# A fused cross-attention and 4-bit feed-forward kernel: order of loads, reciprocals and context transposes within a round

## The reference, cut to what matters

```python
def xattn(q, k, v, Wq, Wk, Wv, Wo, bo, g):            # q = layernorm(x), k = v = ctx, [32, 64, 512]
    qh, kh, vh = heads(Wq @ q), heads(Wk @ k), heads(Wv @ v)      # 8 heads of 64
    qh = softmax(qh, over the head's 64 rows) / 8
    kh = softmax(kh, over the 512 positions)
    context = kh @ vh.T                                # 64 x 64 for each head
    out = Wo @ (context.T @ qh) + bo
    return out / max(norm(out, over the 64 channels), 1e-12) * g * 8

def ffn(x):                                            # 512 -> 1376 -> 512, weights of 4 bits
    gate, up = x @ dequant(Wg), x @ dequant(Wu)
    return (silu(gate) * up) @ dequant(Wd)

x = x + tanh(g_xattn) * xattn(layernorm(x), ctx, ctx, ...)
x = x + tanh(g_ffn) * ffn(layernorm(x))
```

## Time and profile before

| | |
|---|---|
| device time, runs of before | 812.04, 816.8, 819.32 us (median 816.8) |
| the profiled execution | 815.45 us, span 813.7 us from first to last instruction |
| busy: PE, DVE, ACT, POOL | 731.1 us (90%), 612.2 (75%), 436.6 (54%), 186.2 (23%) |
| round 0 begins (first maxima) | at 13.39 us |
| round 1, 2, 3 begin | at 39.48, 65.00, 93.17 us |
| round 15 begins | at 436.31 us |
| feed-forward part, first product | at 523.65 us |
| mean granted TensorE clock | 0.977 of full speed |

### The profile page before, as it was taken

How to read it: one execution, slowest core, us unless ns; L and a number is a source line. 1 busy time by engine, 2 the same in 40 slices (tenths; PEclk the granted TensorE clock), 3 DMA queues, 4 the chain that set the end, 5 groups by cost and what they waited for, 6 DMA issues and landing times. The chain is left out here.

```text
span 813.7 us, 13752 instructions
## 1 busy us (share of the span) xinstructions
PE 731.1 (90%) x4551; PEld 392.8 (48%) x4551; DVE 612.2 (75%) x806; ACT 436.6 (54%) x764; POOL 186.2 (23%) x317
## 2 busy tenths in 40 slices
PE   4889988988998999999999966399999999999997
PEld 3544553554454455455545532135555555555555
DVE  6377776877878777787778554399988877877885
ACT  3766665665666667566665632144443445334443
POOL 5122222213213222321322211211121112211121
PEclk9999999999999999999999996599999999999999
DMA  3021312321330321122020000100000000100001
GB/s 99 9 76 32 81 23 67 81 50 37 80 82 5 82 67 26 48 67 69 11 63 18 5 6 1 63 10 1 1 1 27 27 0 13 39 0 0 26 26 52
DMA packets 29195, 29.89 MB, mean 37 GB/s; under 512 B 18628, under 2 KB 18756, under 8 KB 29036
## 3 DMA queue, kind: packets, MB, share of 16 engines
q1 hardware_dynamic: 26972, 28.85, 13.1%
q10 hardware_dynamic: 2192, 0.66, 0.3%
HBM read 23.49 MB, written 4.23 MB: 34 GB/s over the span
## 5 line engine op out<-in xcount | busy, mean ns | idle before, releaser
L1300 DVE SCALAR_TENSOR_TENSOR acc<-ffn_bank,scale_T,acc 128x512 f32<-128x512 f32 (+1 forms) x264 | 186.7, 748 | 39.6 <-PE ffn_bank L1253 34.1
L1252 PE MATMUL ffn_bank<-ek,w_gu 128*128 (+3 forms) x352 | 137.9, 392 | 2.8 <-PEq L90 1.8
L1253 PE MATMUL ffn_bank<-ekT,w_gu 128*128 (+3 forms) x352 | 134.4, 382 | 0.0
L1160 POOL TENSOR_TENSOR in_lo<-inter,in_hi 128x512 fp32r<-128x512 f32 (+1 forms) x44 | 56.4, 1282 | 229.9 <-ACT in_hi L1199 229.9
L1192 ACT ACTIVATE act_gate<-acc 128x512 f32<-128x512 f32 (+1 forms) x44 | 27.7, 630 | 144.3 <-DVE acc L1300 144.3
L985 DVE TENSOR_TENSOR eq<-eq,pair 128x1024 f32<-128x1024 f32 x64 | 78.0, 1220 | 25.1 <-PE pair L741 25.1
L493 ACT ACTIVATE eq<-pair 128x1024 f32<-128x1024 f32 x64 | 65.6, 1025 | 55.0 <-PE pair L761 55.0
L977 DVE TENSOR_REDUCE qmax<-pair 128x16 f32<-128x1024 f32 x64 | 77.6, 1212 | 14.9 <-PE pair L623 14.6
L484 ACT ACTIVATE ek<-pair,kneg 128x512 f32<-128x512 f32 x128 | 86.6, 685 | 3.6 <-DVE kneg L980 3.5
L1269 PE MATMUL ffn_bank<-wd_hi,in_hi 128*128 128x512 f32 (+1 forms) x176 | 86.7, 531 | 0.4 <-DVE wd_lo L1333 0.4
L1269 PE MATMUL ffn_bank<-wd_lo,in_hi 128*128 128x512 f32 (+1 forms) x176 | 86.7, 531 | 0.0
(11 more groups left out here) (138 smaller groups left out, 1168.7 us busy)
## 6 DMA issues: line engine op xcount, KB each, us to landing
xall<-in_x SPq DMA_DIRECT2D x16, 256.0 KB, 3.9
ctx_raw<-in_ctx SPq DMA_DIRECT2D x16, 256.0 KB, 4.1
out_x<-xall SPq DMA_DIRECT2D x16, 256.0 KB, 2.0
zero<-zeros_plus SPq DMA_DIRECT2D x8, 344.0 KB, 4.0
packed<-in_L_ffn_gate_qweight SPq DMA_DIRECT2D x4, 688.0 KB
packed<-in_L_ffn_up_qweight SPq DMA_DIRECT2D x4, 688.0 KB
packed<-in_L_ffn_down_qweight SPq DMA_DIRECT2D x10, 256.0 KB
d_scale<-in_L_ffn_down_scales SPq DMA_DIRECT2D x1, 1408.0 KB, 6.1
```

The costliest lines, as they stand in the source:

```text
L1252: pe.matmul(gu_bank[job % 4][0:w, :], lhsT, xT_hi[:, g, rows], start=True, stop=False)
L1253: pe.matmul(gu_bank[job % 4][0:w, :], lhsT, xT_lo[:, g, rows], start=False, stop=True).then_inc(gu_mm, 1)
L1300: dve.scalar_tensor_tensor(out=acc[0:w, it % 3, m, :], in0=gu_bank[job % 4][0:w, :], scalar=scale_T[0:w, it, 4 * m + g:4 * m + g + 1], in1 ...
```

## The change

Five pieces of order change; no instruction is added or taken away.

- SyncE: the load of pair p+2 is issued ahead of the weight words.
- TensorE and ScalarE: the context transposes stand behind `k_transposed(0)` in place of the round's end, and the copy of their result (ctxT) behind the first ekT.
- ScalarE: `ctx_high` stands first in the round, ahead of the denominators' copy.
- GpSimd: cs_lo stands ahead of the layernorm moments.
- VectorE: `reciprocals` stands behind maxima(1), ahead of `layernorm_apply`, and ss_max behind the first normalisation.

```diff
--- before.py
+++ after.py
@@ -301,11 +301,11 @@
                     for part in range(2):
                         sp.dma_start(rn_rows[2 * part:2 * part + 2, :].bitcast(F32).rearrange("b (k m) -> b k m", m=8),
                                      rn_parts[:, part, :].bitcast(F32)).then_inc(rn_gathered, 16)
-                if following:
-                    load_weights(p + 1, *following)
                 if project and more:
                     sp.wait_ge(ct_mm, p + 1)
                     load(p + 2, par)
+                if following:
+                    load_weights(p + 1, *following)
 
             step(0, 0, True, False, False)
             step(1, 1, True, True, False, following=(0, 0, 1))
@@ -366,8 +366,8 @@
 
             def step(p, par, residual, following=True):
                 if following:
+                    ctx_low(p + 1, 1 - par)
                     layernorm(p + 1)
-                    ctx_low(p + 1, 1 - par)
                     x_low(p + 1, 1 - par)
                 if residual:
                     inverse_norm(p - 2)
@@ -533,12 +533,12 @@
                     squared_norms()
                     transposed(14, 16)
                     return
+                if not last:
+                    ctx_high(p + 1, i + par, 1 - par)
                 if combine:
                     denominators()
                 k_exp_tile(0, 0)
                 k_exp_tile(0, 1)
-                if not last:
-                    ctx_high(p + 1, i + par, 1 - par)
                 if residual:
                     outputs()
                 k_exp_tile(1, 0)
@@ -558,8 +558,10 @@
                 for t in range(NT):
                     q_exp_tile(t)
                     k_transposed(t)
-                act.wait_ge(ct_mm, p + 1)
-                act.activation(ctxT[:, :, :].rearrange("n t c -> n (t c)"), small[1][:, :], ACT.Copy).then_inc(ct_evac, 1)
+                    if t == 0:
+                        act.wait_ge(ct_mm, p + 1)
+                        act.activation(ctxT[:, :, :].rearrange("n t c -> n (t c)"), small[1][:, :],
+                                       ACT.Copy).then_inc(ct_evac, 1)
 
             def transposed(first, end):
 
@@ -869,6 +871,7 @@
                 spread_reciprocals(0)
                 q_logits(0)
                 k_transposed(0)
+                ctx_transposed()
                 spread_reciprocals(1)
                 q_logits(1)
                 k_transposed(1)
@@ -879,7 +882,6 @@
                 spread_reciprocals(3)
                 q_logits(3)
                 k_transposed(3)
-                ctx_transposed()
 
             step(0, 0, 0, True, False, False)
             step(1, 0, 1, True, True, False)
@@ -1000,26 +1002,27 @@
                     if not last:
                         layernorm_stats(p + 1, i + par, 1 - par)
                     maxima(1)
+                    if combine:
+                        reciprocals()
                     if not last:
                         layernorm_apply(p + 1)
                     maxima(2)
+                    maxima(3)
                 if drain:
                     ffn_input(*((0, 4) if combine else (12, 14)))
-                if combine:
-                    reciprocals()
-                if project:
-                    maxima(3)
+                    if combine:
+                        reciprocals()
                 if isinstance(p, int) and p == 0:
                     gates()
                 if drain and combine:
                     ffn_input(4, 8)
-                if residual:
-                    dve.wait_ge(ss_spread, 32 * (r2 + 1))
-                    dve.tensor_scalar(ss_max[:, :], ss_sq[:, :], 1e-24, None, ALU.max).then_inc(ss_bounded, 1)
                 if weights:
                     nibbles(p, *weights)
                 if combine:
                     normalise(0)
+                if residual:
+                    dve.wait_ge(ss_spread, 32 * (r2 + 1))
+                    dve.tensor_scalar(ss_max[:, :], ss_sq[:, :], 1e-24, None, ALU.max).then_inc(ss_bounded, 1)
                 if combine:
                     dve.wait_ge(m_mm, r + 1)
                     dve.wait_ge(kinv_ready, r + 1)
```

## The result

The changed kernel takes 788.38 us (median of four runs, 788.29 to 788.89), the kernel before 815.54 beside it (812.04 to 819.32): ratio 0.967, 95% interval 0.962 to 0.971. The forecast was 790 us, with a range of 781 to 806. The profiled execution took 788.89 us, span 787.1.

A forecast was written before the change was run, and what follows sets the result against it. TensorE was taken as nearly the bound in rounds 3 to 14, its gaps made by late VectorE. Steady rounds -28.7, round 0 +3.5, ends -1.0 gave -26.2 us: 790 us, range 781 to 806.

The forecast's parts named there:

- The steady rounds: Rounds 3 to 14: each falls from 28.6 to 26.2 us, -28.7 us over the twelve.
- The anchor: Rounds 3 to 14: TensorE's busy time alone needs 26.2 us a round, so nothing less can be had.
- The added wait: VectorE, reciprocals behind maxima(1): idles some 0.75 us for den_sq, taken to land 4.10 us after its issue.
- a wait of over 1 us: Sign that the forecast is wrong: the reciprocals wait over 1 us for den_sq, where 0.5 to 1 was expected.
- cs_lo ahead of the moments: GpSimd, steady rounds: cs_lo ends near T+1.4, beside qmax(0), so VectorE's xn takes 0.55 us instead of 1.61.
- Round 0: First round: moments wait behind cs_lo, xn at about 24.3 instead of 20.87; +3.5 us in the sum.
- The ends: Rounds 1 and 2, last round and drain: together -1.0 us, between -3 and +1, an estimate.
- C: Pair lands 4.7 us into the next round, delaying the denominators' copy behind ctx_high: rounds 30.0, 836 us; chance 0.08.
- B: Weight words ahead of the den_sq spread delay its landing to T+8 from T+6.05: rounds 28.0, 811 us; chance 0.12.
- A: VectorE's front: xn keeps 1.61 us by meeting other GpSimd work, or den_sq lands 1 us later: 801 us; chance 0.18.

## Why the prediction was right, and where it was not

The parts build on each other, and the runs give a staircase of steady rounds:

| kernel | steady round | step |
|---|---|---|
| before | 28.60 | |
| + load order | 27.74 | -0.86 |
| + context transposes | 27.29 | -0.45 |
| + ctx_high first, ss_max later | 26.93 | -0.36 |
| + reciprocals early | 26.15 | -0.78 |
| + GpSimd order | 26.14 | 0, and +3 us in round 0 |

The third step holds two moves, and no run separates them. The traces of its two kernels do in part: xn starts at T+5.5 in both and the wait for the gathered reciprocals is 9.2 and 9.3 us, while the 34.5 us of waiting for ss_sq and TensorE's 3.4 for eq are gone. So the ss_max move is seen at work there, and a gain from ctx_high is not shown.

Undone one at a time in the changed kernel, the load order costs 51.2 us, the transposes 23.1, ctx_high 10.0, the reciprocals 7.2, the GpSimd order -3.2 and ss_max 0.3, which sum to far more than the 27 us of the change. The load order and the transposes are two conditions for one thing, that the pair is there when ScalarE turns to it.

**The steady rounds** were right, by the steps given. Forecast 26.2, measured 26.14; 12 rounds gave -29.4 against -28.7. t_logits(3) came at T+9.06 (forecast T+8.98), spread(0) at T+14.26 (T+14.2), spread(1) at T+17.08 (T+17.1), spread(3) at T+22.09 (T+22.1). The anchor, TensorE's busy time as the floor of the round, held: 312.27 of 313.80 us.

**The added wait** was 1.1 us where the forecast said 0.75. den_sq was issued at T+2.04 (T+1.95) and used 4.21 us later (4.10 taken from rden_rows). It cost nothing, since VectorE still reached maxima(2) in time. The prediction had named a wait of over 1 us as a sign that it was wrong. That sign came up with the rest right, so the bound was set too tight.

**cs_lo ahead of the moments** is the step that failed, and its number came true by luck. The prediction said "in the new order cs_lo is done near T+1.4 ... So xn takes 0.55". xn did take 0.55, and does so with the old order too. What frees it is the reciprocals ahead of it, with their wait: in the old GpSimd order cs_lo runs from T+5.55 to T+6.83 and xn starts at T+7.34. By the prediction's own numbers this could have been seen. It had put xn at T+7.1, and the earlier trace rows have cs_lo at T+8.0 only because the stats were 2.4 us late then.

**Round 0** was right: xn at 24.20 (forecast 24.3), +3.14 us (3.5).

**The ends** were put at -1.0 and gave -0.3. Rounds 1 and 2 were not walked through. Round 1 lost 1.57 us. In it the reciprocals wait 2.12 us for den_sq, twice the steady wait, TensorE then stands for 2.75 us, and its products slow down. Round 2 and the end of the program gave 1.13 and 0.8 back.

**The rivals.** C was measured: 839.5 where it said 836, but with the words ahead of the load, which the change doesn't have, and with 19 us of slower products in it that C didn't count. Less these, the rounds would take about 28.9 us (an estimate, 365.95 less 19.4 over twelve) and not C's 30.0, so the near match of 839.5 and 836 is in part luck. B's mechanism exists, but is smaller: with the words 3 us ahead of it den_sq took 5.07 us, so 0.9 us more and not 2. In the changed kernel the words go 6.2 us ahead of den_sq (249.61, against the next round's start at 253.75 + 2.04) and it takes 4.21. A's collision exists too, and returns as soon as the reciprocals stand late, at xn or at the cast.

## What to carry to other kernels

Read what a stage could take at best from the busy time of its busiest engine, and check a gain against that floor. When a load is moved forward, move with it what frees its buffer, and don't let an earlier engine's queue wait for it unless it has landed: with the pair there, ctx_high at the head of ScalarE's queue was worth 10 us to a GpSimd order that has cs_lo ahead of the moments, and with the pair late it passed the delay on to all else. Walk through the first rounds of a pipeline by themselves; a hand-written order that is best in the steady rounds cost 6.6 us in the first two, and can be written otherwise there.

## What the hardware showed that was not expected

**VectorE beside GpSimd.** The cast of 128x64 elements takes 0.19 us alone, 0.72 and 1.24 beside xs_lo; xn takes 0.55 alone and 1.60 beside cs_lo. The maxima, 1.21 us, are no longer when cs_lo runs beside them (227.57 against 227.59 on GpSimd in the changed kernel). The Trainium skill, page "SBUF — State Buffer", section "Who interferes with whom", counts cast and tensor_scalar among the operations that can take the port pair shared with GpSimd, holds that one side then blocks fully, and excepts tensor_reduce. These runs agree: the held cast ends 0.05 and 0.06 us behind xs_lo, the held xn 0.27 behind cs_lo, GpSimd's instruction keeps its 1.28 us, and the reductions keep theirs. The starts don't tell which side is held, since xn starts 0.05 us ahead of cs_lo and is held even so. What was new is that such a collision can wander: an edit that frees one instruction drives another one into it.

**TensorE's pace behind a gap.** In the changed kernel the products after the 2.75 us gap of round 1 take 0.79 us for 0.50, at a granted clock of 0.50 from 53 to 56 us, the lower of the clock's two levels (1.2 GHz for 2.4). The two experiments that share this start (the words first, ss_max back) show it at the same place. With GpSimd's old order the gap is as long and nothing happens, and with ctx_high back the gap is longer and nothing happens either:

```profile
49.59 0.50 PE L625 MATMUL pair<-wqT_hi,xs_hi 64*128 64x512 f32 x2 [2.76 <-DVE qmax L979]
```

```profile
53.80 0.50 PE L625 MATMUL pair<-wqT_hi,xs_hi 64*128 64x512 f32 x2 [3.15 <-DVE qmax L979]
```

Round 1 took 25.52 us with GpSimd's old order and 27.09 in the changed kernel, so the lower pace cost about 1.6 us, as much as the gap itself did (25.52 against 23.89 with the reciprocals late). The kernel with the words first meets it in its steady rounds too. Ten of its twelve gaps ahead of t_logits(3), of 2.12 to 2.82 us, are followed by a granted clock of 0.50 within 2 us, and the two shorter ones, of 1.83 and 2.00, are not. So there the gap goes with the fall, but the gap alone doesn't bring it, as the two rows above show. What else decides is open. The time at which TensorE first reached its full pace doesn't tell them apart: 31.6 us with GpSimd's old order and 35.4 with ctx_high back, where the clock stayed up, and 35.6 in the changed kernel, where it fell.

**The start scatters.** Nearly the same first round took 26.09 us in the kernel before and 23.47 in the one with load order and transposes, mostly because the products reached the higher pace at 31.9 us in the one and by 27.05 in the other. The pace is read from their lengths (0.79 and 0.66 us against 0.50 and 0.40); the granted clock can't decide it there, for it reads 1.00 at 24 to 31 us in the kernel before and 0.50 at the same time with GpSimd's old order, with products of nearly the same lengths. So a single profile can't tell a gain of 2 us in round 0. The 3 us of the GpSimd order rest on more: round 0 took 28.2 to 29.7 us in all six profiles of kernels with that order there, and 23.5 to 26.2 in all six without it. A chance start of this kind may also stand behind the 5 to 7 us between runs of one kernel; that was not tested.
